# GpSimd makes six chunks' numerator sums, and its products and two chunks' scans change places

## What is computed

```python
ek = jnp.exp(jnp.minimum(kf, 30.0))
ekv = ek * vf
...
a = a * decay + ekv_t
b = b * decay + ek_t
...
euk = jnp.exp(jnp.minimum(u.astype(jnp.float32)[None, None, :] + kf, 30.0))
num = nf + nb - ekv + euk * vf
den = df + db - ek + euk
base = jax.nn.sigmoid(r.astype(jnp.float32)) * (num / jnp.maximum(den, 1e-08))
out = base * (0.8 + 0.2 * tf)
```

## Time and profile before

| | us |
|---|---|
| median of 3 runs (885.30 to 887.55) | 886.83 |
| the profiled execution | 886.21 |
| its span | 884.5 |
| mean granted TensorE clock, as a share of full | 0.941 |
| busy in the span: PE / DVE / ACT / POOL | 754.4 / 578.6 / 437.1 / 235.0 |
| layer 0 / layer 1 / layer 2 start at | 0 / 147.3 / 270.6 |

### The profile page before, as it was taken

The page is one execution under the profiler, slowest core; times in us unless marked ns, Lnnn a source line. Parts: engine busy times, 40 slices in busy tenths (PEclk is TensorE's granted clock), DMA queues, the critical chain, the costliest instruction groups (busy, mean ns, idle before and its releaser), DMA issues.

```text
span 884.5 us, 11278 instructions
## 1 busy us (share of the span) xinstructions
PE 754.4 (85%) x3633; PEld 571.6 (65%) x3633; DVE 578.6 (65%) x1290; ACT 437.1 (49%) x878; POOL 235.0 (27%) x241
## 2 busy tenths in 40 slices
PE   1886685978785537899999999999989899999997
PEld 0433452734443126678888888898877688888885
DVE  5998899879997986775576566755684233322333
ACT  5895452234423556655555555654655243343342
POOL 5310112320140440021111021200121355455453
PEclk9999898789896877999999999999999999999998
DMA  4000002923222000210110101101001622213321
GB/s 152 2 1 1 0 0 84 402 73 103 88 62 87 1 0 1 96 48 1 49 49 1 49 1 49 38 1 36 2 3 51 189 60 83 80 40 84 84 56 47
DMA packets 37422, 49.84 MB, mean 56 GB/s; under 512 B 18574, under 2 KB 29942, under 8 KB 35702
## 3 DMA queue, kind: packets, MB, share of 16 engines
q1 hardware_dynamic: 36310, 46.90, 16.7%
q0 software_dynamic: 768, 2.10, 0.7%
q10 hardware_dynamic: 288, 0.14, 0.1%
HBM read 42.99 MB, written 6.13 MB: 56 GB/s over the span
## 4 chain that ended last, share of the span: by engine, by line
PE 56%; DVE 8%; ACT 3%; issue 1%; POOL 1%; DVEq 0%; ACTq 0%
PE bank L2014 15%; PE bank L2591 9%; PE bank L2030 8%; PE bank L2606 5%; PE bank L2586 5%; PE bank L2665 3%; PE bank L2682 3%; PE bank L2672 2%; PE bank L2664 1%; PE bank L2683 1%; PE bank L1627 1%; PE bank L1730 1%; DVE PN L2488 1%; PE bank L1654 1%; DVE H L1544 1%
## 5 line engine op out<-in xcount | busy, mean ns | idle before, releaser
L2058 DVE TENSOR_TENSOR B_l<-bank,TW_l 128x512 f32<-128x512 f32 (+1 forms) x50 | 34.5, 690 | 133.9 <-PE bank L2014 133.9
L2225 POOL TENSOR_TENSOR WL<-RAW,WH 128x512 fp32r<-128x512 f32 x28 | 36.0, 1286 | 221.1 <-ACT WH L2258 221.1
L2083 POOL TENSOR_TENSOR HL_l<-H_l,HH_l 128x512 fp32r<-128x512 f32 (+1 forms) x50 | 64.9, 1298 | 111.5 <-ACT HH_l L2075 111.5
L2317 ACT ACTIVATE EX<-EX,nm 128x128 f32<-128x128 f32 (+1 forms) x128 | 57.0, 447 | 67.2 <-DVE nm L2479 67.2
L2067 ACT ACTIVATE S_l<-bank 128x512 f32<-128x512 f32 (+1 forms) x50 | 29.9, 599 | 85.4 <-PE bank L2014 85.3
L159 POOL TENSOR_TENSOR WV<-EUK,V 128x512 f32<-128x512 f32 x16 | 23.8, 1498 | 152.5 <-DVE GAIN L288 89.8
L2493 DVE TENSOR_TENSOR AL<-bank,AH 128x256 fp32r<-128x256 f32 x64 | 27.0, 424 | 53.9 <-ACT AH L2331 53.9
L2591 PE MATMUL bank<-XH,WH 128*128 128x512 f32 x128 | 58.6, 458 | 0.7 <-DVE XL L1779 0.7
L2014 PE MATMUL bank<-XH,WH 128*128 128x512 f32 (+1 forms) x136 | 54.5, 401 | 0.0
L2014 PE MATMUL bank<-XL,WH 128*128 128x512 f32 (+1 forms) x136 | 54.0, 397 | 0.0
L2014 PE MATMUL bank<-XH,WL 128*128 128x512 f32 (+1 forms) x136 | 53.8, 396 | 0.0
(11 more groups left out here) (322 smaller groups left out, 2197.2 us busy)
## 6 DMA issues: line engine op xcount, KB each, us to landing
RAW<-l_attn SPq DMA_DIRECT2D x8, 1024.0 KB, 4.8
WE<-l_experts SPq DMA_DIRECT2D x1, 6144.0 KB, 24.5
...
```

What stands on the lines that cost most here:

```text
L2083: pool.tensor_tensor(self.HL[0:rows, q % 4], self.H[0:rows, q % 2], self.HH[0:rows, q % 4].bitcast(F32), ALU.subtract).then_inc(self.h_low, 1)
L2317: act.activation(EX[:, s, a:b], EX[:, s, a:b], ACT.Exp, bias=nm[:, s, i:i + 1], scale=scale, accum_out=rs[:, s, i:i + 1]).then_inc(expd, 1)
```

## The change

1. `OWN_NUM = (7, 9, 10, 11, 12, 13)`: for these six chunks VectorE's `add` has only the two sums of the denominator. GpSimd makes the two of the numerator (`gain_pool_num`), behind them on a new semaphore g_num, and VectorE waits for it before GAIN. g_add's counts are now worked out by `gain_adds`.
2. On GpSimd the product of c = 8 goes from layer 1's start to layer 0's end, that of c = 9 behind the scatter, and that of c = 15 behind the gather. Where the chunk two before has its sums on GpSimd, a product waits for these and not for the gain.
3. The pieces of VectorE are laid out anew: c = 10's `den` and `num` stand between the shared expert and the first tile (FETCH1 = 2), the loop has 15 pieces, one a tile, and c = 15's `den` and `num` stand at the end of layer 1 (END1 = 5) and no longer in layer 2.

No instruction is added but for these moves: VectorE has twelve sums fewer, GpSimd twelve more.

The diff (the semaphore's line, and three places where only the count of g_add or the call of `numerator` is put in, are left out):

```diff
--- before.py
+++ after.py
@@ -151,12 +152,32 @@
 def gain_pool(pool, k, c):
 
     layer, j = gain_layer(c)
-    if c >= 2:
-
+    if c - 2 in OWN_NUM:
+        pool.wait_ge(k.g_num, 2 * OWN_NUM.index(c - 2) + 2)
+    elif c >= 2:
         pool.wait_ge(k.g_done, c - 1)
 
     pool.wait_ge(k.capped, 2 + layer)
     pool.tensor_tensor(k.WV[:, c % 2], chunk(k.EUK[layer][:], j), chunk(k.V[:], j), ALU.mult).then_inc(k.g_w, 1)
+
+
+
+OWN_NUM = (7, 9, 10, 11, 12, 13)
+
+
+def gain_pool_num(pool, k, c):
+
+    s, n = gain_slot(c), 2 * OWN_NUM.index(c)
+    pool.wait_ge(k.g_add, gain_adds(c + 1))
+    pool.tensor_tensor(k.NF[s][:], k.NF[s][:], k.NB[s][:], ALU.add).then_inc(k.g_num, 1)
+    pool.wait_ge(k.g_num, n + 1)
+    pool.wait_ge(k.g_w, c + 1)
+    pool.tensor_tensor(k.NF[s][:], k.NF[s][:], k.WV[:, c % 2], ALU.add).then_inc(k.g_num, 1)
+
+
+def gain_adds(c):
+
+    return sum(2 if i in OWN_NUM else 4 for i in range(NCH, c))
 
 
 def gain_den(pe, k, c, den):
@@ -236,21 +257,29 @@
     def add(self):
 
         v, k, c, s = self.v, self.k, self.c, self.slot
-        n = 4 * (c - gain_sum_no(c))
+        n, own = gain_adds(c), c in OWN_NUM
         v.wait_ge(k.g_scan, 8 * c + 8)
         v.tensor_tensor(k.DF[s][:], k.DF[s][:], k.DB[s][:], ALU.add).then_inc(k.g_add, 1)
-        v.tensor_tensor(k.NF[s][:], k.NF[s][:], k.NB[s][:], ALU.add).then_inc(k.g_add, 1)
+        if not own:
+            v.tensor_tensor(k.NF[s][:], k.NF[s][:], k.NB[s][:], ALU.add).then_inc(k.g_add, 1)
         v.wait_ge(k.capped, 2 + self.layer)
         v.wait_ge(k.g_add, n + 1)
         v.tensor_tensor(k.DF[s][:], k.DF[s][:], chunk(k.EUK[self.layer][:], self.j), ALU.add).then_inc(k.g_add, 1)
+        if own:
+            return
         v.wait_ge(k.g_w, c + 1)
         v.wait_ge(k.g_add, n + 2)
         v.tensor_tensor(k.NF[s][:], k.NF[s][:], k.WV[:, c % 2], ALU.add).then_inc(k.g_add, 1)
 
+    def numerator(self):
+
+        if self.c in OWN_NUM:
+            self.v.wait_ge(self.k.g_num, 2 * OWN_NUM.index(self.c) + 2)
+
     def reciprocal_of(self, half):
 
         v, k, c, s = self.v, self.k, self.c, self.slot
-        v.wait_ge(k.g_add, 4 * (c - gain_sum_no(c)) + 4)
+        v.wait_ge(k.g_add, gain_adds(c + 1))
         at = slice(half * SEQ, (half + 1) * SEQ)
         v.reciprocal(k.DF[s][:, at], k.DF[s][:, at]).then_inc(k.g_rec, 1)
 
@@ -284,7 +314,7 @@
         if gain_summed(c):
             v.wait_ge(k.g_sum, 2 * gain_sum_no(c) + 2)
         v.wait_ge(k.g_rec, c + 1)
-
+        self.numerator()
         v.scalar_tensor_tensor(chunk(k.GAIN[:, self.layer % 2], self.j), k.DF[s][:], 1e8, num,
                                ALU.min, ALU.mult).then_inc(k.g_done, 1)
 
@@ -486,6 +516,8 @@
                 pool.tensor_tensor(chunk(k.EKV[:], j), chunk(k.EK[:], j), chunk(k.V[:], j), ALU.mult).then_inc(k.g_ekv, 1)
             for c in range(2 * NCH):
                 gain_pool(pool, k, c)
+            gain_pool_num(pool, k, 2 * NCH - 1)
+            gain_pool(pool, k, 2 * NCH)
 
         @block.scalar
         def _(act):
@@ -898,13 +930,13 @@
 PIECES = list(gain_pieces())
 
 
-LOGITS1, RANKS1, START1, MIDDLE1, END1 = 2, 1, 5, 17, 3
-FIRST_PIECE2 = LOGITS1 + RANKS1 + START1 + MIDDLE1 + END1
+LOGITS1, RANKS1, START1, FETCH1, MIDDLE1, END1 = 2, 1, 5, 2, 15, 5
+FIRST_PIECE2 = LOGITS1 + RANKS1 + START1 + FETCH1 + MIDDLE1 + END1
 
 
 def pieces_after(j):
 
-    at = LOGITS1 + RANKS1 + START1
+    at = LOGITS1 + RANKS1 + START1 + FETCH1
     return PIECES[at + MIDDLE1 * j // TILES1:at + MIDDLE1 * (j + 1) // TILES1]
 
 
@@ -1067,8 +1099,6 @@
                                pattern=[[1, P]], channel_multiplier=-1).then_inc(consts, 1)
             for j in range(TILES1):
                 pool.memset(TILE[:, j], float(j)).then_inc(consts, 1)
-            for c in range(FIRST_GAIN1, FIRST_GAIN1 + 2):
-                gain_pool(pool, k, c)
 
             pool.wait_ge(zeroed, 16)
             pool.wait_ge(pos, 10)
@@ -1077,8 +1107,10 @@
                 pool.wait_ge(xtok, t + 1)
                 pool.indirect_dma_start(xs_d, bass.IndirectOffsetOnAxis(ap=SLOT[:, t:t + 1], axis=0), XTOK[:, t],
                                         None).then_inc(scat, 16)
-            for c in range(FIRST_GAIN1 + 2, LAYERS * NCH):
+            for c in range(FIRST_GAIN1 + 1, LAYERS * NCH - 1):
                 gain_pool(pool, k, c)
+                if c in OWN_NUM:
+                    gain_pool_num(pool, k, c)
             for n in range(RING1):
 
                 pool.wait_ge(y_out[n], 16 * len(range(n, TILES1, RING1)))
@@ -1086,6 +1118,7 @@
             for t in range(NT):
                 pool.indirect_dma_start(YG[:, t], None, ys_d, bass.IndirectOffsetOnAxis(ap=SLOT[:, t:t + 1], axis=0)
                                         ).then_inc(y_in[t], 16)
+            gain_pool(pool, k, LAYERS * NCH - 1)
 
         @block.scalar
         def _(act):
@@ -1205,6 +1238,8 @@
                 v.wait_ge(s_silu, q + 1)
                 v.tensor_tensor(HS[:, q], SS[:, q % 2], shared_banks[q % 2][1][:], ALU.mult).then_inc(s_h, 1)
                 gain_pieces_done(v, k, PIECES[at + q:at + q + 1])
+            at += 4
+            gain_pieces_done(v, k, PIECES[at:at + FETCH1])
             for j in range(TILES1):
 
                 v.wait_ge(silu, j + 1)
@@ -1577,9 +1612,8 @@
                 hidden(t)
                 if t >= 2:
                     maxima(t - 2)
-                gain_pieces_done(v, k, rest[t:t + 1] if t < 2 else [])
             maxima(EARLY2 - 2)
-            gain_pieces_done(v, k, rest[2:3])
+            gain_pieces_done(v, k, rest[0:1])
             maxima(EARLY2 - 1)
             factors(0)
             for u in range(LATE2):
```

More of the change, by code:

```diff
@@ L110, in make_gain @@
     k.g_add = sem("g_add")
+    k.g_num = sem("g_num")
     k.g_rec = sem("g_rec")
@@ L194, in gain_scalar @@
     act.wait_ge(k.g_done, c)
[L195 removed]
+    act.wait_ge(k.g_add, gain_adds(c) + (2 if c in OWN_NUM else 3))
     act.activation(k.RC[:], k.DF[gain_slot(c)][:], ACT.Ln).then_inc(k.g_log, 1)
```

1 line of the change is left out of this document (removed).

## The result

| | before | changed |
|---|---|---|
| median of 4 runs, us | 887.19 | 875.56 |
| lowest and highest | 885.30, 887.84 | 873.79, 876.07 |
| the profiled execution; its span | 886.21; 884.5 | 873.79; 872.1 |
| mean granted TensorE clock | 0.941 | 0.947 |
| busy PE / DVE / ACT / POOL | 754.4 / 578.6 / 437.1 / 235.0 | 752.6 / 562.7 / 437.2 / 246.8 |

The account below looks back on a forecast made before the run. VectorE was taken to bound most stretches, with the RAW fetch as the tile loop's second limit; 1.0 + 1.4 + 0.6 + 0 + 0.5 + 7.5 = 11.0 us gave a forecast of 875.8 us, range 869.5 to 881.5.

Parts of the forecast that it names:

- Layer 0's end: End of layer 0: two of chunk 7's sums leave VectorE, gain 1.0 us, bounds 0.6 and 1.2.
- Entry of layer 1: Start of layer 1: products of chunks 8 and 9 no longer run beside XC, gain 1.4 us, bounds 1.0 and 1.5.
- Scatter: Layer 1's eight indirect DMAs: two of VectorE's four sums beside them go, gain 0.6 us, between 0 and 1.7.
- Tile loop: Layer 1's fifteen tiles: VectorE's saving becomes fetch wait, gain 0; bounds 4 us later and 12.6 earlier.
- first rival: Tile loop follows VectorE: in full 12.6 us more gain, 863.2; half of it, 869.5; chance 0.14.
- 12.6 us less work: Tile loop: VectorE's work falls by 9.6 us of scans and sums plus three stalls of about 1 us.
- second limit: Tile loop: ScalarE waits 2.42 us for RAW, the next ternary weights, fetched only after the previous are rounded and written out.
- GpSimd's lateness: Rival: GpSimd's three jobs take 5.1 us against a reciprocal's 3.35, GAIN waits; 886.4, or 881 half hidden; chance 0.06.
- No GAIN waits more than 0.3 in the loop: Sign expected in the changed profile's tile loop: GAIN is held up by at most 0.3 us.
- Gather: End of layer 1: the gather no longer stands behind chunk 15's product, gain 0.5 us, bounds 0 and 1.7.
- some 3.5 us: End of layer 1: VectorE's idle cover before layer 2 expected to remain, from 4.25 us before.
- Layer 2: Layer 2's first six tiles: without chunk 15's scans GpSimd's H products set the pace, gain 7.5 us, bounds 6.5 and 8.0.

Follow-up runs that it names:

- before_c15_alone: The kernel before with only chunk 15's eight scans moved from layer 2 to the end of layer 1; 880.42 us, ratio 0.9931.
- magnitudes_later: The changed kernel with magnitudes and rounding of the second and third ternary matrix one tile later; 869.46 us, ratio 0.9830.

## Why the prediction was right, and where it was not

**Layer 0's end, 1.0.** Right: 1.03 on its own. The other 1.1 of the -2.11 was no part of the change; it is the low clock that the profiled execution of the kernel before happened to have. What the prediction didn't say is that chunk 8's product has to stand behind chunk 7's sums on GpSimd: ahead of them it costs a scan 0.7.

**Entry of layer 1, 1.4.** Right: 1.41, and given back exactly when the products return.

**Scatter, 0.6.** Too small: 1.67, the upper bound. The step that failed is "nearer to the bottom, because the other long one is only 0.4 above the short one". The two lengths were not of one kind. The steady 0.3 to 0.45 more is there beside any scans, in every kernel. The other 1.7 came only beside chunk 9's four sums, and went as a whole when two of them left. The way to the first HT gave 0.4 back, as the scans in front of it allowed (0.7 at most). The rule of the Trainium skill that was weighed here ("SBUF — State Buffer", section "Who interferes with whom": no contention of two-input VectorE work with the writing of descriptors) would have forecast 0; the runs show otherwise.

**Tile loop, 0.** Right for the most part. The loop is 1.3 shorter in the profile, but six runs with the same work for TensorE and VectorE in it (the changed kernel and five experiments that leave it alone) have 57.1 to 59.0, and the kernel before had 58.4 in one profile, 59.4 in before_c15_alone. Its reasons hold: the fetch wait grew from 2.4 to 6.8, the fourth HT came 11.69 behind the first where it was 10.90, and the first was 0.42 late, 1.2 in all (forecast 1.5), and stretches at the low clock followed two of the three waits. That the fetch is the limit is shown by taking its wait away (4.8 us), and that it was not the limit before by the same edit there (nothing). What the prediction had wrong is the size of the first rival: "12.6 us less work" counts what leaves the loop but not chunk 13's division, 4.0 us, which the same text moves ahead of the last HT. It leaves 8.6; 7.8 were measured. The full rival would have been 867, not 863. The loop came near it in magnitudes_later only (6.1 less than before), once the second limit was gone.

**GpSimd's lateness.** Its instructions stayed at 1.26 to 1.28 beside the reciprocal. GAIN took 0.43 longer once ahead of the loop (chunk 9) and 0.12 once in it (chunk 10), each time beside the next product, and 0.69 otherwise. "No GAIN waits more than 0.3 in the loop" holds.

**Gather, 0.5.** The sum was near (0.3), its reason wrong. "It stood behind the product of chunk 15": it stood behind the last result's transfer, which ended at about the same time as the product. From the end of the last YO to the first DMA it is 3.26 in the kernel before and 3.27 in the changed one, and moving the product back in the changed one changes nothing. (For the kernel before it is read from this distance and wasn't tried.) What does change the time there is VectorE's work: chunk 15's scans cost 0.8, and against before_c15_alone the other parts give back 1.16 (21.99 to 20.83), presumably because chunk 13's division is out of the way: there VectorE itself ended the layer. The cover of "some 3.5 us" was 4.29.

**Layer 2, 7.5.** Right: 7.33 in the profile, 7.6 and 7.3 when put back or made alone. GpSimd sets the pace after it, one product every 2.53 to 3.0 us.

The total is 11.6 against 11.0 by the medians, 12.4 by the two profiles. The largest terms, 7.5, 1.4 and 1.0, were right with their mechanism. That the rest comes out so near is luck in part: layer 0's 1.1 of clock, the scatter's missing 1.1 and the loop's 1.3 lie on the one side; on the other the way to the first HT, the start of layer 2 and the layers behind it gave back 0.4, 0.4 and 1.0. The 0.4 at the start of layer 2 doesn't belong to the change: magnitudes_later, with the same instructions there, has the 15.85 of the kernel before. In the changed profile the granted clock was 0.50 from 270.5 to 280.5, where the other two had 0.63 to 0.92, and VectorE waits 1.42 for ScalarE's S instead of 1.01; that the one comes of the other was not tried. What the last 1.0 is made of was not tried either.
